# Second attention's front: query and key rows kept token-major, squared and summed on VectorE, normalised along the row, then turned to features

## The chip, the cores and the metric

The kernel runs on one core of a Trainium2 chip. The metric is the device time of one execution in microseconds (us). Engines are written as the profile writes them: PE is TensorE (PEld its weight loads), DVE is VectorE, ACT is ScalarE, POOL is GpSimd, SP is SyncE, which here only issues DMAs.

## The reference, cut to what matters

Two transformer layers run over an input of 8 batches x 512 tokens x 256 features. The change touches only the second layer's attention, with 16 heads of 16 features:

```python
def _rms_norm(x, w):
    ms = jnp.mean(jnp.square(x), axis=-1, keepdims=True)
    return x * jax.lax.rsqrt(ms + EPS) * w
...
xh = x.reshape(b, t, H, HD).transpose(0, 2, 1, 3)
c_q = jnp.einsum('bhtd,ld->bhtl', xh, W_DQ)
q_c = jnp.einsum('bhtl,dl->bhtd', c_q, W_UQ)
q_c_norm = _rms_norm(q_c, q_norm_w)
...
k_c_norm = _rms_norm(k_c, k_norm_w)
k_r = jnp.einsum('bhtd,rd->bhtr', xh, W_KR)
...
scores = jnp.einsum('bhqd,bhkd->bhqk', q, k) * scale
```

The rotary weights are folded into the key side beforehand, so that one query row of 16 features and one key row of 16 features (normalised key plus a linear term of x) give the scores. The mean in the norm goes over the 16 features of one head and one token.

## The kernel before, in words

The second layer (function `layer1`) walks a common list of **slots**. Slot n computes the scores of head n (128 heads, n = 0 to 127), and exponentials, the product with the values and the output of earlier heads. Every engine has its own program, written in slot order, and runs it strictly in that order; engines wait for each other by semaphores.

Beside the heads runs the **front**: front f (16 of them, one for 8 heads of one batch) makes queries, keys and values for 8 heads. Its steps are spread over slots: step s of front f stands in slot 8f - 23 + s (`front_at`, LEAD = 23), so one step of some front with the same remainder by 8 stands in each slot. In the text "slot 4" is a slot that holds step 4 (and step 12 of the front before it). Fronts 0 to 2 stand mostly in slots below 0, where there are no heads yet.

The steps that matter, before the change (a = 0 is the query, a = 1 the key):

- step -2, `turn`, `features`: PE turns x to feature-major, ACT copies it to `xs`.
- steps 1 and 2, `project`: one matmul with 512 columns from fixed weights to `ps_b` (features on partitions, tokens along the row); ACT copies it out (`keep`, to `raw_q` / `raw_k`) and squares it (`square`, to `sq`).
- steps 3 and 5, `squares`: four matmuls against the 128x8 matrix `mean8` give the mean square of each token and head, tokens on partitions; DVE adds the epsilon (`means`, L1988).
- POOL, `root`: to the power -1/2, 16 numbers a partition at a time; step 4 and 5 for the query's two halves, 6 and 7 for the key's. `widen` (steps 5 and 7) copies each root to its head's 16 columns in `roots`.
- `spread_roots` (step 7 query, step 12 key): PE turns `roots` to feature-major in `ps_a`; DVE multiplies (`normed`, L1995, same slots). `rotary` (step 12) adds the key's linear term.
- `high` (ACT) and `low` (DVE) split query (steps 8 and 9) and key (step 13) into a high and a low word; SP writes them out (`spread`) and gathers them by head (`fill`).
- `values` (step 9): PE makes the values from `xs` and may start when the query's multiply is done.

In each slot POOL first cuts the upper triangle from an earlier head's exponentials (`cut`, L1551: two instructions, the second waits for ACT's last exponential of that slot). In each slot DVE first takes the maxima of the slot's four score tiles (`mask_max`, L2019); PE's scores of the next slot wait for them tile by tile. In slots 2 and 6 DVE then runs `outputs` (L2029 to L2036), and PE's `attend` in the following slot (3 or 7) waits for its second instruction. In slots 3 and 8 (until batch 7 is done) DVE runs `mix` (L1974 to L1981), and POOL issues the gathers for it.

## Time and profile before

| | us |
|---|---|
| median of 3 runs | 1800.76 (1798.89 to 1802.2) |
| the profiled execution | 1813.85 |
| its span in the trace | 1812.1 |
| second attention with fronts beside the heads | about 1116 to 1490 of the span |
| busy share of the whole span | PE 91%, DVE 66%, ACT 56%, POOL 30% |

The trace is one execution; its times are microseconds from the start of the span. The busy share of PE is modelled from pipelined matmuls, so durations that follow each other closely overlap; where a cost of PE is wanted, the distance from one start to the next is used.

### The profile page before, as it was taken

Reading aid. Unit: us, or ns where it says so; the run is one execution under the profiler, and the core shown is the slowest. Engines: PE = TensorE matmul, PEld = TensorE weight load, DVE = VectorE, ACT = ScalarE, POOL = GpSimd, SP = SyncE. Lnnn points to the kernel's source line nnn. Section 1 sums busy time; section 2 is a strip of 40 time slices with the busy share of each in tenths; the row PEclk is TensorE's granted clock in tenths of the full one; section 3 lists DMA queues with packets and bytes.
Section 4 is the critical chain, followed back from the end, with each engine's and each line's share of the span. In section 5 each row is a group of like instructions: output and inputs, shape, how many; then the busy total and the mean of one; then the engine's idle time right before and its main releaser. Section 6 shows DMA issues by size and latency. Waiting matters only on the chain. (4 is left out here: it accounts for less than half of the span.)

```text
span 1812.1 us, 30114 instructions
## 1 busy us (share of the span) xinstructions
PE 1646.1 (91%) x9124; PEld 1131.0 (62%) x9125; DVE 1204.8 (66%) x4166; ACT 1013.9 (56%) x2528; POOL 550.7 (30%) x683
## 2 busy tenths in 40 slices
PE   6899999999999999978688877899999988899996
PEld 4667676767676767654577645566666664466665
DVE  1797878787878788727444445778888776134245
ACT  1676767676767676624233362566667665652430
POOL 1000101010101010101444288789988763200001
PEclk9999999999999999989799986899999998999998
DMA  4211111111111111120244426888877777000000
GB/s 109 71 30 47 41 47 42 48 42 47 41 48 37 49 39 36 36 93 1 82 136 135 113 64 130 141 141 133 137 131 133 117 123 118 1 6 18 18 24 29
DMA packets 82766, 128.35 MB, mean 71 GB/s; under 512 B 14784, under 2 KB 40848, under 8 KB 82496
## 3 DMA queue, kind: packets, MB, share of 16 engines
q1 hardware_dynamic: 71232, 100.11, 27.1%
q0 software_dynamic: 9664, 25.93, 6.0%
q8 instruction: 71, 1.16, 0.3%
q10 hardware_dynamic: 1728, 0.55, 0.2%
q14 instruction: 71, 0.58, 0.1%
HBM read 73.59 MB, written 35.65 MB: 60 GB/s over the span
## 5 line engine op out<-in xcount | busy, mean ns | idle before, releaser
L413 ACT ACTIVATE c_probs<-c_probs,a_negmax 128x128 f32<-128x128 f32 (+3 forms) x512 | 279.6, 550 | 0.0
L1867 ACT ACTIVATE c_probs<-a_ps_st 128x384 f32<-128x384 f32 (+1 forms) x384 | 189.9, 526 | 134.0 <-PE a_ps_st L1667 129.6
L418 ACT ACTIVATE c_probs<-a_ps_trans 128x512 f32<-128x512 f32 (+1 forms) x256 | 124.7, 487 | 215.0 <-PE a_ps_trans L331 214.0
L2019 DVE CUSTOM_DVE_ANT_0 a_junk<-a_ps_score,c_mask 128x128 f32<-128x128 f32 (+3 forms) x512 | 220.3, 486 | 35.4 <-PE a_ps_score L1645 28.5
L473 DVE CUSTOM_DVE_ANT_0 c_probs<-a_ps_score,c_mask 128x128 f32<-128x128 f32 (+3 forms) x512 | 219.6, 485 | 19.8 <-PE a_ps_score L315 18.7
L536 POOL TENSOR_SCALAR a_rstd<-a_mv 128x4 f32<-128x4 f32 x8 | 1.8, 230 | 705.8 <-DVE a_mv L503 705.8
L331 PE MATMUL a_ps_trans<-c_ident,c_probs 128*128 128x128 f32 x1280 | 188.6, 278 | 17.7 <-DVE c_probs L490 16.1
L331 PEld LDWEIGHTS a_ps_trans<-c_ident,c_probs 128*128 128x128 f32 x1280 | 147.1, 141 | 87.4 <-issue 39.3
L1501 POOL TENSOR_TENSOR a_ms<-a_ms,c_minus_half 128x16 f32<-128x16 f32 x64 | 187.4, 2931 | 1.8 <-DVE a_ms L1988 1.8
L1667 PE MATMUL a_ps_st<-a_qs,a_ks 128*128 128x512 f32 (+3 forms) x512 | 155.4, 365 | 26.4 <-ACT c_probs L1867 14.4
L314 PE MATMUL a_ps_score<-a_kh,a_qs 128*128 128x128 f32 (+3 forms) x512 | 167.4, 351 | 7.0 <-issue 4.6
L490 DVE TENSOR_SCALAR c_probs<-c_probs,a_recip 128x128 f32<-128x128 f32 (+3 forms) x512 | 164.3, 384 | 4.5
L315 PE MATMUL a_ps_score<-a_kl,a_qs 128*128 128x128 f32 (+3 forms) x512 | 165.3, 323 | 0.0
L344 PE MATMUL a_ps_y<-c_probs,a_latv 128*64 128x512 f32 (+3 forms) x1024 | 153.1, 441 | 0.5 <-ACT c_probs L418 0.5
L1667 PEld LDWEIGHTS a_ps_st<-a_qs,a_ks 128*128 128x128 f32 x512 | 88.2, 193 | 86.5 <-ACT c_probs L1867 45.7
L1551 POOL TENSOR_SCALAR_AFFINE_SELECT c_probs<-c_probs 128x256 f32<-128x256 f32 x256 | 104.1, 422 | 112.1 <-ACT c_probs L1867 111.7
L465 DVE TENSOR_TENSOR a_qlow<-a_ps_q,a_qs 64x512 fp32r<-64x512 f32 x128 | 88.1, 689 | 73.9 <-ACT a_qs L407 71.4
L297 PE MATMUL a_ps_q<-a_xT,a_wqk 128*128 128x512 f32 x256 | 123.0, 603 | 0.0
L1645 PE MATMUL a_ps_score<-a_ks,a_qs 128*128 128x128 f32 (+3 forms) x512 | 117.6, 351 | 2.1 <-DVE a_negmax L2019 1.6
L344 PEld LDWEIGHTS a_ps_y<-c_probs,a_latv 128*64 128x64 f32 x1024 | 68.1, 137 | 81.0 <-issue 70.7
L371 PE MATMUL a_ps_kv<-a_wvo,a_yT 128*128 128x256 f32 x464 | 105.1, 379 | 0.7 <-ACT a_yT L432 0.7
L314 PEld LDWEIGHTS a_ps_score<-a_kh,a_qs 128*128 128x128 f32 x512 | 97.5, 190 | 12.0 <-issue 9.4
(265 smaller groups left out, 3143.4 us busy)
## 6 DMA issues: line engine op xcount, KB each, us to landing
a_qs<-a_qlow SPq DMA_DIRECT2D x128, 128.0 KB, 2.2
bounce<-a_words SPq DMA_DIRECT2D x64, 256.0 KB, 2.0
a_qs<-bounce SPq DMA_DIRECT2D x128, 128.0 KB, 5.7
a_ks<-bounce SPq DMA_DIRECT2D x128, 128.0 KB, 6.3
slot_out<-m_y SPq DMA_DIRECT2D x80, 128.0 KB, 1.7
a_xT<-in_xT SPq DMA_DIRECT2D x8, 512.0 KB
c_X<-in_x SPq DMA_DIRECT2D x8, 512.0 KB
token_rows<-c_X SPq DMA_DIRECT2D x8, 512.0 KB, 5.7
```

The source lines that it names most:

```text
L314: pe.matmul(to, q, kh[b % 2][:, 0:keys], start=True, stop=False)
L315: last = pe.matmul(to, q, kl[b % 2][:, 0:keys], start=False, stop=True)
L331: last = pe.transpose(ps_trans[(3 * n + grp) % 2][:, col:col + P], prob[:, n % 4, QOFF[i] + P * k:QOFF[i] + P * (k + 1)], C.ident[:])
L344: last = pe.matmul(ps_y[LD * c:LD * (c + 1), P * k:L], latv[g // NPAIR % 2][:, k, :], probT[:, (2 * g + c) % 4, at:at + L - P * k], start= ...
L413: act.activation(at, at, ACT.Exp, scale=-1.0, bias=negmax[:, n % 4, i:i + 1], accum_out=rowsum[:, n % 4, i:i + 1]).then_inc(s_exp, 1)
L418: act.activation(probT[:, n % 4, TGCOL[grp]:TGCOL[grp] + TGLEN[grp]], ps_trans[(3 * n + grp) % 2][:, 0:TGLEN[grp]], ACT.Copy).then_inc(s_p ...
L473: dve.tensor_tensor_reduce(out=prob[:, n % 4, QOFF[i]:QOFF[i] + keys], in0=ps_score[grp][:, SCOL[i]:SCOL[i] + keys], in1=C.mask[:, L - key ...
L490: dve.tensor_scalar(at, at, recip[:, n % 4, i:i + 1], None, ALU.mult).then_inc(s_norm, 1)
L1501: pool.tensor_tensor(at, at, C.minus_half[:, 0:2 * HH], ALU.pow).then_inc(s_root, 1)
L1667: last = pe.matmul(ps_st[item % 2][:, col:col + KLEN[c]], KS[u % NQ][:, j, P * c:P * (c + 1)], QS[u % NQ][:, j, P * c:L], start=True, stop ...
L1867: act.activation(probT[:, r8, col:col + width], ps_st[item % 2][:, 0:width], ACT.Exp).then_inc(s_stc, 1)
L2019: dve.tensor_tensor_reduce(out=junk[:, to:to + keys], in0=ps_score[g][:, at:at + keys], in1=C.mask[:, L - keys:L], scale=-1.0, scalar=3.0e ...
```

## The change

Query and key are now projected with tokens on the partitions: `project` uses the four tiles of `xs` as weights and streams the 128 columns of the weight matrix. ACT copies and squares as before, now scaled by 1/4 so that a sum is a mean. `means` is a `tensor_reduce` over 16 columns on DVE. The epsilon moves to POOL, one `tensor_scalar` ahead of each power. `widen`, `squares` and the matrix `mean8` go away. `normed` multiplies along the row in place in `raw_q` / `raw_k`, with the root broadcast over 16 columns; PE then turns the product (`turn_normed`). ACT makes the query's high word straight from `ps_a` with the norm weight as scale, DVE the low word; for the key ACT writes the weighted tile (`weigh`), DVE adds the rotary term.

In slots: `normed` of the query moves on DVE from 7 to 6, that of the key from 12 to 8; `low` of the query from 9 to 8; the key's `means` from 5 to 4; `high` of the query on ACT from 8 to 7; `weigh` is new in 12. `normed` waits for both halves of POOL's roots; `turn_normed` waits for `normed`; `values` now waits for `low` of the query.

```diff
                 def root(f, a, half):
-                    pool.wait_ge(s_msc, f * 2 + a + 1)
                     at = ms[:, a, 2 * half:2 * half + 2, :].rearrange("p t h -> p (t h)")
+                    pool.wait_ge(s_ms, f * 2 + a + 1)
+                    pool.tensor_scalar(at, at, RMS_EPS, None, ALU.add).then_inc(s_root, 1)
+                    pool.wait_ge(s_root, 8 * f + 4 * a + 2 * half + 1)
                     pool.tensor_tensor(at, at, C.minus_half[:, 0:2 * HH], ALU.pow).then_inc(s_root, 1)
...
+                def project(f, a):
+                    if a:
+                        pe.wait_ge(s_rawc, 2 * f + 1)
+                    else:
                         pe.wait_ge(s_xs, f + 1)
...
+                    for t in range(TT):
+                        last = pe.matmul(ps_b[:, P * t:P * (t + 1)], xs[f % 2][:, P * t:P * (t + 1)],
+                                         w[:, (SQ, SK)[a], :], start=True, stop=True)
+                    last.then_inc(s_raw, 1)
...
                 def values(f):
-                    pe.wait_ge(s_fin, 2 * f + 1)
+                    pe.wait_ge(s_lo, 2 * f + 1)
...
+                def turn_normed(f, a):
+                    pe.wait_ge(s_nrm, f * 2 + a + 1)
...
+                        last = pe.transpose(ps_a[:, P * t:P * (t + 1)], raw(f, a)[:, P * t:P * (t + 1)], C.ident[:])
                     last.then_inc(s_bc, 1)
...
+                        act.activation(words[0][:], ps_a[:], ACT.Copy, scale=qk_norm[:, 0:1]).then_inc(s_hi, 1)
...
+                def weigh(f):
+                    act.wait_ge(s_bc, 2 * f + 2)
...
+                    act.activation(fin, ps_a[:], ACT.Copy, scale=qk_norm[:, 1:2]).then_inc(s_kw, 1)
...
                 def means(f, a):
...
+                    dve.wait_ge(s_sq, f * 2 + a + 1)
+                    dve.tensor_reduce(ms[:, a, :, :].rearrange("p t h -> p (t h)"),
+                                      sq[:, a, :].rearrange("p (n d) -> p n d", d=HD), AX.X, ALU.add
+                                      ).then_inc(s_ms, 1)
 
                 def normed(f, a):
...
+                    dve.wait_ge(s_root, 8 * f + 4 * a + 4)
+                    at = raw(f, a)[:].rearrange("p (t h d) -> p t h d", t=TT, h=HH)
+                    dve.tensor_tensor(at, at, ms[:, a, :, :].unsqueeze(3).to_broadcast([P, TT, HH, HD]),
+                                      ALU.mult).then_inc(s_nrm, 1)
...
                     if front_at(n, 3) is not None:
                         means(front_at(n, 3), 0)
                     if front_at(n, 12) is not None:
-                        normed(front_at(n, 12), 1)
                         rotary(front_at(n, 12))
-                    if front_at(n, 5) is not None:
-                        means(front_at(n, 5), 1)
-                    if front_at(n, 7) is not None:
-                        normed(front_at(n, 7), 0)
-                    if front_at(n, 9) is not None:
-                        low(front_at(n, 9), 0)
+                    if front_at(n, 4) is not None:
+                        means(front_at(n, 4), 1)
+                    if front_at(n, 6) is not None:
+                        normed(front_at(n, 6), 0)
+                    if front_at(n, 8) is not None:
+                        normed(front_at(n, 8), 1)
+                        low(front_at(n, 8), 0)
```

What stands in a row on DVE from the end of slot 6's maxima on, before (each "128x512" row of `c_mask` is the last tile of a slot's maxima, the first tiles are left out; `a_raw_q` is the query, `a_raw_k` the key, `a_got` the mix):

```order
L2019 ISA a_junk,a_negmax<-a_ps_score,c_mask 128x512
...
L2029 RECIPROCAL a_recip<-a_ps_y 128x16
L2031 TENSOR_TENSOR a_yq<-a_ps_y,a_recip 128x256
L2036 TENSOR_TENSOR c_X<-c_X,a_yq 128x4x64
...
L1995 SCALAR_TENSOR_TENSOR a_sq<-a_raw_q,c_qk_norm,a_ps_a 128x512
L2043 BN_STATS a_stats<-c_X 128x6
...
L1974 SCALAR_TENSOR_TENSOR c_X<-a_got,c_weight,c_X 128x256 x2
```

The same stretch of DVE after the change:

```order
L2001 ISA a_junk,a_negmax<-a_ps_score,c_mask 128x512
...
L1977 TENSOR_TENSOR a_raw_q<-a_raw_q,a_ms 128x512
L2011 RECIPROCAL a_recip<-a_ps_y 128x16
L2013 TENSOR_TENSOR a_yq<-a_ps_y,a_recip 128x256
L2018 TENSOR_TENSOR c_X<-c_X,a_yq 128x4x64
...
L2025 BN_STATS a_stats<-c_X 128x6
...
L1977 TENSOR_TENSOR a_raw_k<-a_raw_k,a_ms 128x512
L1936 SCALAR_TENSOR_TENSOR a_words<-a_ps_a,c_qk_norm,a_words 128x512
L1959 SCALAR_TENSOR_TENSOR c_X<-a_got,c_weight,c_X 128x256 x2
```

The query's multiply now stands ahead of slot 6's `outputs`, and the key's multiply and the query's low word stand between slot 8's maxima and its mix.

POOL from slot 4 to slot 8, before:

```order
L1501 TENSOR_TENSOR a_ms<-a_ms,c_minus_half 128x16
L1551 AFFINE_SELECT c_probs<-c_probs 128x2x128 x2
L1501 TENSOR_TENSOR a_ms<-a_ms,c_minus_half 128x16
L1507 COPY a_roots<-a_ms 128x512
L1551 AFFINE_SELECT c_probs<-c_probs 128x2x128 x4
```

and after:

```order
L1499 TENSOR_SCALAR a_ms<-a_ms 128x16
L1501 TENSOR_TENSOR a_ms<-a_ms,c_minus_half 128x16
L1543 AFFINE_SELECT c_probs<-c_probs 128x2x128 x2
L1499 TENSOR_SCALAR a_ms<-a_ms 128x16
L1501 TENSOR_TENSOR a_ms<-a_ms,c_minus_half 128x16
L1543 AFFINE_SELECT c_probs<-c_probs 128x2x128 x4
```

This is the key's half (slots 6 to 8); the query's reads alike. The copy after two powers is gone, and each power has an addition ahead of it.

## Rows read from the trace of the kernel before

**Rows 1.** Windows view: stretch, length, busy us (instructions), PEclk, DMA share, GB/s
```profile
1200.00:1300.00 100.00, 93.49 (x669) 61.62 (x668) 82.98 (x321) 67.51 (x142) 88.86 (x108) 1.00 0.83 135
```
**Rows 2.** Windows view of PE alone: stretch, length, busy us (instructions), PEclk, DMA share, GB/s
```profile
1504.00:1508.00 4.00, 2.38 (x10) 0.85 0.61 101
1508.00:1512.00 4.00, 4.00 (x20) 0.73 1.11 123
```
**Rows 3.** Waits view from 1165 to 1480: us in total, times, longest us
```profile
PEld a_ps_a L1633 <- POOL a_roots L1507: 19.7, 12, 1.8
```
**Rows 4.** Chain of work that ended last, merged: start us, us, what
```profile
1286.69 0.89 PE a_ps_a L1602 x8
1287.58 0.86 PE a_ps_b L1596 x2
...
1294.98 0.79 PE a_ps_a L1617 x8
```
**Rows 5.** Timeline of POOL: start us, us, instruction xcount [idle before <-releaser]
```profile
1070.15 5.82 POOL L1501 TENSOR_TENSOR a_ms<-a_ms,c_minus_half 128x16 f32<-128x16 f32 x2
...
1083.14 0.59 POOL L1524 TENSOR_SCALAR a_crstd<-a_cmv 128x4 f32<-128x4 f32 x1
...
1291.00 0.23 POOL L1524 TENSOR_SCALAR a_crstd<-a_cmv 128x4 f32<-128x4 f32 x1
1291.32 1.04 POOL L1526 TENSOR_TENSOR a_crstd<-a_crstd,c_minus_half 128x4 f32<-128x4 f32 x1
...
1301.33 2.94 POOL L1501 TENSOR_TENSOR a_ms<-a_ms,c_minus_half 128x16 f32<-128x16 f32 x1
...
1304.98 2.90 POOL L1501 TENSOR_TENSOR a_ms<-a_ms,c_minus_half 128x16 f32<-128x16 f32 x1
1307.94 0.61 POOL L1507 COPY a_roots<-a_ms 128x512 f32<-128x512 f32 x1
...
1313.02 3.06 POOL L1501 TENSOR_TENSOR a_ms<-a_ms,c_minus_half 128x16 f32<-128x16 f32 x1
```
**Rows 6.** Timeline of DVE, slots 6 to 9
```profile
1306.01 0.42 DVE L2031 TENSOR_TENSOR a_yq<-a_ps_y,a_recip 128x256 f32<-128x256 f32 x1
...
1309.30 0.75 DVE L1995 SCALAR_TENSOR_TENSOR a_sq<-a_raw_q,c_qk_norm,a_ps_a 128x512 f32<-128x512 f32 x1 [0.59 <-PE a_ps_a L1633]
1309.97 0.42 DVE L2043 BATCH_NORM_STATS2 a_stats<-c_X 128x6 f32<-128x256 f32 x1
...
1310.54 0.29 DVE L2019 CUSTOM_DVE_ANT_0 a_junk<-a_ps_score,c_mask 128x128 f32<-128x128 f32 x1
...
1312.19 1.14 DVE L1974 SCALAR_TENSOR_TENSOR c_X<-a_got,c_weight,c_X 128x256 f32<-128x256 f32 x2
...
1313.94 0.29 DVE L2019 CUSTOM_DVE_ANT_0 a_junk<-a_ps_score,c_mask 128x128 f32<-128x128 f32 x1
...
1315.59 0.69 DVE L1951 TENSOR_TENSOR a_words<-a_sq,a_words 128x512 fp32r<-128x512 f32 x1
1316.20 0.42 DVE L2043 BATCH_NORM_STATS2 a_stats<-c_X 128x6 f32<-128x256 f32 x1
```
**Rows 7.** Timeline of PE: slot 2's scores, slot 7's attend, then slots 8 to 10
```profile
1288.89 0.85 PE L1645 MATMUL a_ps_score<-a_ks,a_qs 128*128 128x128 f32 x4
...
1306.70 1.07 PE L1683 MATMUL a_ps_y<-c_probs,a_v 128*32 128x512 f32 x8
...
1308.61 0.66 PE L1633 MATMUL a_ps_a<-c_ident,a_roots 128*128 128x128 f32 x4 [0.84 <-POOL a_roots L1507]
...
1309.28 0.85 PE L1645 MATMUL a_ps_score<-a_ks,a_qs 128*128 128x128 f32 x4
...
1312.69 0.86 PE L1645 MATMUL a_ps_score<-a_ks,a_qs 128*128 128x128 f32 x4
...
1313.79 1.05 PE L1602 MATMUL a_ps_a<-c_w,a_xs 128*128 128x128 f32 x8
...
1316.15 0.85 PE L1645 MATMUL a_ps_score<-a_ks,a_qs 128*128 128x128 f32 x4
```

146 lines of the change are left out of this document (51 added, 95 removed).

## The prediction, as it was put on record

> **What bounds the kernel now.** I read the windows first, then the waits, the chain of work, and the timelines of POOL, DVE and PE over one front's period. From 1200 to 1300, beside the heads, PE is busy 93.49 of 100 us, POOL 88.86, DVE 82.98 and ACT 67.51, at a full PE clock [rows 1]. Three engines are near their limit, so what counts is who waits for whom in order. One front with its eight heads takes 27.26 us: slot 2's scores start at 1288.89, and those of slot 10 (the next slot 2) at 1316.15 [rows 7]. PE is the bound most of the time, but the period closes through POOL: between 1165 and 1480 PE's weight loads stand 19.7 us, 12 times, for the widened roots [rows 3]. POOL's four powers are the long piece: each is 2.9 us, they start at 1301.33, cannot start earlier (they stand behind a cut that waits for slot 4's last exponential), and the last one ends at 1313.02 + 3.06 = 1316.08 [rows 5]. That is the time at which PE is already in slot 10. Nobody minds today, because the key's roots are used only in slot 12.
>
> **PE.** Removed per front: two `squares` of 0.79 us [rows 4]. Two projections of 0.86 us become eight token tiles; their nearest row is `values`, four tiles of the same shape in 0.89 us [rows 4], so +0.03 each. The turns stay eight transposes. Sum: 1.58 - 0.06 = 1.52 us less on PE a front, 24 us in 16 fronts, if PE stays the bound.
>
> **POOL.** The addition ahead of each power costs 0.32 us from start to start, by the addition of 4 numbers that stands at 1291.00 ahead of a power at 1291.32 [rows 5]; with 16 numbers it may be 0.4. The copy that goes cost 1308.52 - 1307.94 = 0.58 plus 0.06 ahead of it (the copy starts at 1307.94 behind a power at 1304.98 of 2.90, the next cut follows it directly [rows 5]). Four additions, two copies: 1.28 against 1.28, nothing, at worst +0.3. Counted from the start of the first power's addition (R), the query's roots are ready at 0.32 + 2.92 + 0.73 (a cut of two instructions: 1304.98 - 1301.33 - 2.92 [rows 5]) + 0.32 + 2.88 = 7.2, the key's at 4 x 3.22 + 3 x 0.76 = 15.15.
>
> **DVE's own work.** `means` grows from 0.11 (start to start, 128x32) to about 0.6: not shown before; bounds 0.43 (half the elements) and 0.75, nearest row a 512-element operation, 0.61 from start to start (1315.59 to 1316.20 [rows 6]). `normed` shrinks from 0.67 (1309.97 - 1309.30) to 0.61, `low` of the query grows from 0.61 to 0.67. Together +0.95 us a front. DVE is idle 17 of 100 us, 4.6 a front, so this work alone costs nothing; if it fell on the path in full it would be 13 x 0.95 = 12. ACT gets `weigh`, 0.6 us in slot 4; it is idle 32 of 100 us [rows 1], nothing either.
>
> **DVE's new place in the order.** Here the time is decided. DVE runs in order, and `normed` now waits for POOL inside the stream of maxima on which PE's scores depend. I take R = 1301.33 and give times after R.
>
> Slot 6: DVE is through with its maxima at 4.4 (`outputs` begins with a reciprocal 0.28 ahead of 1306.01) and waits until 7.2 for the query's roots. Behind it stand `outputs`, whose second instruction PE's `attend` in slot 7 wants. Before it started at 1306.01, ended at 1306.43, and `attend` started at 1306.70 [rows 6, 7]: there was no slack at all. Now 7.2 + 0.61 + 0.74 = 8.55 and `attend` starts 3.2 us later than its 5.37. One thing comes back: the 0.84 us for which the turn at 1308.61 waited. From `attend` to slot 8's scores it was 1309.28 - 1306.70 = 2.58, without that wait 1.7 [rows 7]; slot 8's scores start at 10.2 instead of 7.95.
>
> Slot 8: DVE takes slot 7's maxima from 9.05 to 10.7, statistics 0.57 (1310.54 - 1309.97), slot 8's maxima 1.65 (1312.19 - 1310.54 [rows 6]) to 12.9, and then waits for the key's roots until 15.2. `normed` to 15.8, `low` to 16.5, the mix 1.75 (1313.94 - 1312.19) to 18.2, slot 9's maxima to 19.85. PE: slot 9's scores at 10.2 + 3.41 = 13.6, `values` could start 1.10 later, at 14.7 (1313.79 - 1312.69 [rows 7]), but waits for `low` until 16.5: 1.8 us. From `values` to slot 10 it is 1316.15 - 1313.79 = 2.36: slot 10 at 18.9, where its last tile waits for the last maximum at 19.9. That equals a start at 19.5 without waits. Before it was 1316.15 - 1301.33 = 14.8. So the stretch from the roots to slot 10 is 4.7 us longer while there is a mix, 4.1 without.
>
> The rest of the period, slot 2's scores to the next R, was 1301.33 - 1288.89 = 12.44 and loses one `squares`: 11.65. Period 19.5 + 11.65 = 31.15, **3.9 us more than 27.26**; without the mix 3.3. The other `squares` (slot 5) and PE's 1.5 us are swallowed by the waits.
>
> **Sum.** Fronts 4 to 12 have the mix and a full period: 9 x 3.9 = 35. Fronts 13 and 14: 2 x 3.3 = 7. Front 15 pays 4.1 and has no next one. Front 3, whose last two powers stand behind the first cuts, pays 4.4 - 0.8 = 3.6. Ahead of the heads the same wait delays the mix: front 0's powers start at 1070.15, four of 3.22 end at 1083.05, then 0.61 + 0.67 + 1.6 (mix) bring the statistics to 1086.0, for which POOL waits with what began at 1083.14 [rows 5]: 2.9 us. Front 2 does it again and holds up slots 2 to 4, about 3 more: 6, between 2 (PE waits for a DMA ahead of slot 7's exponents, which could hide most of it) and 9. Together 35 + 7 + 4.1 + 3.6 + 6 = **56 us**. The profiled execution would go from 1813.85 to 1870; the median of the runs lies 13.1 lower, so 1800.76 + 56 = **1857**.
>
> **A rule beside it.** POOL's power was 2.90 us in most rows and 3.06 beside the mix at 1312.19, a DVE instruction with two inputs from SBUF [rows 5, 6]. The new `normed` of the query is another such instruction and meets POOL's cut and third power: by 3.06 - 2.90 some 0.15 us a front, 2 us in all. The Trainium skill (GPSIMD Engine Reference, section Key points) says that GPSIMD shares its SBUF interfaces with VectorE and contends with instructions that have two SBUF inputs; by that rule the sum would be 58 instead of 56. I keep 56.
>
> **The rivals.**
> *A, the clock (22%).* With 7 us of PE waits in a period of 31, PE's clock may fall. In a stretch of 4 us of the trace before in which PE was busy for 2.38, the granted clock was 0.85, and 0.73 in the next 4, PE being partly at 1.2 instead of 2.4 GHz [rows 2]: (0.15 + 0.27) x 4 = 1.7 us lost. Once a front on the path: 13 x 1.7 = 22, 1879. Against it: half of the waits stand ahead of PE work that has slack until `low`. The Trainium skill (TensorE: Matmul & The Clock Gate, section HAM oscillation) warns that waits between bursts of matmuls make the clock fall again each time; by it this rival would be the likely one.
> *B, partly absorbed (14%).* PE reaches slot 4 early enough that the pattern settles with 1.5 to 2.5 us a front: 13 x 2 + 3 = 29, 1830. It needs slots 10 to 12 to run faster than before; DVE's 0.95 us speak against it.
> *C, faster (7%).* DVE's waits never reach PE and PE's relief counts: 1801 - 24 = 1777. The point that decides: the key's roots must be ready when DVE is through with slot 8's maxima. Before that was at 1312.19, and POOL's last power ended at 1316.08: 3.9 us too late, with POOL no faster than before.
> *D, no difference (5%).* The new waits cost just the 1.5 us a front that PE saves, 1801.
> The forecast has 52%.
>
> **How the numbers follow.** Predicted is the likeliest case, 1857, whose own range is 1843 to 1871 (the startup from 2 to 9, the addition, the reduce, the mix). The range takes in rival A and the upper half of B: 1832 to 1885. A measurement of this kernel can tell about 0.2%, 3.6 us. Faster: C and a little, 0.08. Same: 0.05. Slower: 0.87.
>
> **What would show it.** In the profile after: DVE waiting for POOL at `normed`, about 2.8 us in slot 6 and 2.3 in slot 8 of each front; PE waiting ahead of `attend` in slot 7 (3.2 us) and ahead of `values` (1.8); the distance between two fronts' first powers 31 us with the mix; POOL idle longer ahead of slot 4's cut; PE busy below 80 of 100 us between 1200 and 1300. Wrong it would be if DVE found the roots ready (the roots' place on POOL moved forward), if the reduce took over 1.2 us (DVE would be the bound), or if slots 10 to 12 ran at a different pace. A granted clock well below 1.00 there speaks for A.

## The result, and the profile after

| | before | after |
|---|---|---|
| median, first chip | 1799.83 us (4 runs, 1797.65 to 1802.2) | 1884.84 us (4 runs, 1883.24 to 1888.08) |
| ratio, 95% interval | | 1.0474 (1.0458 to 1.0489) |
| ratio, second chip (a0_again) | 1812.16 us | 1897.48 us, 1.0465 (1.0447 to 1.0482) |
| span of the profiled execution | 1812.1 us | 1886.4 us |

The change makes the kernel 4.7% slower: 85 us, where 56 was forecast (1857, range to 1885). Against the 1800.76 of the prediction the ratio gives 1886.1, a hair outside the range. The sign and the waits were as predicted; the size was a third too small, mainly because TensorE's clock was taken as staying full.

Two stretches of the windows view of the profile after; the columns are those of [rows 1].

```profile
core 0: us, PE busy (x) PEld busy (x) DVE busy (x) ACT busy (x) POOL busy (x), PEclk, DMA share, GB/s
1200.00:1300.00 100.00, 80.70 (x555) 52.68 (x548) 72.35 (x265) 57.15 (x118) 74.49 (x93) 0.91 0.68 114
...
1400.00:1500.00 100.00, 78.67 (x520) 53.45 (x519) 68.61 (x257) 57.16 (x119) 66.97 (x85) 0.90 0.59 101
```

From 1200 to 1300 every engine does less than in [rows 1] (PE 93.49, DVE 82.98, ACT 67.51, POOL 88.86), and the granted clock is 0.91 where it was 1.00. No engine has become the bound. They wait for one another.

Who waits for whom, from 1165 to 1540 (us in total, times, longest). There are 11 rounds of a front here.

```profile
POOL c_probs L1543 <- ACT c_probs L1847: 91.7, 58, 5.3
...
PE a_ps_y L1661 <- DVE a_yq L2013: 41.6, 11, 4.8
DVE a_raw_q L1977 <- POOL a_ms L1501: 34.6, 11, 4.1
DVE a_raw_k L1977 <- POOL a_ms L1501: 28.4, 11, 3.1
...
PE a_ps_a L1598 <- DVE a_words L1936: 14.7, 11, 1.7
```

Rows three and four are the new ones: VectorE stands 3.1 us a front at the query's roots and 2.6 us at the key's (forecast 2.8 and 2.3). Row two is what follows: TensorE's `attend` waits 3.8 us a front for the outputs that are queued behind the first of these waits. Row five is the values' wait for the low half. In [rows 3] the longest of TensorE's waits for roots was 1.8 us.

One front in the timelines of POOL, DVE and PE, beside [rows 5 to 7]. The first power's addition starts at 1203.44; times "after R" are counted from there.

```profile
1203.44 0.26 POOL L1499 TENSOR_SCALAR a_ms<-a_ms 128x16 f32<-128x16 f32 x1
1203.78 2.94 POOL L1501 TENSOR_TENSOR a_ms<-a_ms,c_minus_half 128x16 f32<-128x16 f32 x1
1206.70 0.76 POOL L1543 TENSOR_SCALAR_AFFINE_SELECT c_probs<-c_probs 128x256 f32<-128x256 f32 x2
...
1207.78 2.94 POOL L1501 TENSOR_TENSOR a_ms<-a_ms,c_minus_half 128x16 f32<-128x16 f32 x1
1210.69 1.21 POOL L1543 TENSOR_SCALAR_AFFINE_SELECT c_probs<-c_probs 128x256 f32<-128x256 f32 x2
...
1212.21 2.93 POOL L1501 TENSOR_TENSOR a_ms<-a_ms,c_minus_half 128x16 f32<-128x16 f32 x1
1215.11 0.41 POOL L1543 TENSOR_SCALAR_AFFINE_SELECT c_probs<-c_probs 128x256 f32<-128x256 f32 x1
1216.62 0.41 POOL L1543 TENSOR_SCALAR_AFFINE_SELECT c_probs<-c_probs 128x256 f32<-128x256 f32 x1 [1.10 <-ACT c_probs L1847]
...
1217.34 2.93 POOL L1501 TENSOR_TENSOR a_ms<-a_ms,c_minus_half 128x16 f32<-128x16 f32 x1
1220.24 1.21 POOL L1543 TENSOR_SCALAR_AFFINE_SELECT c_probs<-c_probs 128x256 f32<-128x256 f32 x2
```

```profile
1210.75 0.88 DVE L1977 TENSOR_TENSOR a_raw_q<-a_raw_q,a_ms 128x512 f32<-128x512 f32 x1 [2.94 <-POOL a_ms L1501]
...
1211.83 0.42 DVE L2013 TENSOR_TENSOR a_yq<-a_ps_y,a_recip 128x256 f32<-128x256 f32 x1
...
1220.30 0.88 DVE L1977 TENSOR_TENSOR a_raw_k<-a_raw_k,a_ms 128x512 f32<-128x512 f32 x1 [2.30 <-POOL a_ms L1501]
1221.11 0.74 DVE L1936 SCALAR_TENSOR_TENSOR a_words<-a_ps_a,c_qk_norm,a_words 128x512 fp32r<-128x512 f32 x1
```

```profile
1212.40 1.93 PE L1661 MATMUL a_ps_y<-c_probs,a_v 128*32 128x512 f32 x8 [3.58 <-DVE a_yq L2013]
1214.27 1.12 PE L1611 MATMUL a_ps_a<-c_ident,a_raw_q 128*128 128x128 f32 x4
...
1215.50 1.48 PE L1623 MATMUL a_ps_score<-a_ks,a_qs 128*128 128x128 f32 x4
...
1221.90 1.16 PE L1598 MATMUL a_ps_a<-c_w,a_xs 128*128 128x128 f32 x8 [0.75 <-DVE a_words L1936]
...
1224.41 0.62 PE L1623 MATMUL a_ps_score<-a_ks,a_qs 128*128 128x128 f32 x3
```

The query's roots end at 1210.72, 7.3 after R. VectorE, idle for 2.94 us, starts at once. The second instruction of the outputs ends at 1212.25 and `attend` starts at 1212.40. In slot 7 POOL's second cut waits 1.10 us for ScalarE's exponential (1216.62), so the key's roots end at 1220.27, 16.8 after R. The low half ends at 1221.85 and the values start at 1221.90. The scores of slot 10 start at 1224.41, 21.0 after R; before, it was 14.8 from the first power [rows 5, 7].

The granted clock of the same stretch, in the windows view of PE alone (length, busy us, PEclk, DMA share, GB/s):

```profile
1204.00:1208.00 4.00, 3.36 (x22) 1.00 0.38 139
1208.00:1212.00 4.00, 0.82 (x4) 0.90 0.95 141
1212.00:1216.00 4.00, 3.60 (x16) 0.50 1.04 120
1216.00:1220.00 4.00, 4.00 (x34) 0.74 0.23 73
```

TensorE was busy for 0.82 of the 4 us from 1208 to 1212. In the next four the clock is 0.50 (1.2 instead of 2.4 GHz) and then 0.74. That is why `attend` takes 1.93 us here instead of 1.07, the turn 1.12 instead of 0.66 and the scores 1.48 instead of 0.85. The Trainium skill (TensorE: Matmul & The Clock Gate, section HAM oscillation) says that waits between bursts of matmuls make the clock fall again each time; this trace agrees: from front 4 to front 15, `attend` in slot 7 takes 1.86 to 1.94 us in each of the twelve rows. It is not so in every trace. In a0_again, the same kernel run once more, one of these rows takes 1.49 us, and two (fronts 6 and 11) are at full speed, behind waits of 2.27 us:

```profile
1251.77 1.06 PE L1661 MATMUL a_ps_y<-c_probs,a_v 128*32 128x512 f32 x8 [2.27 <-DVE a_yq L2013]
```

Fronts 11 to 13 have a second fall, behind the values' wait (PE timeline of front 12):

```profile
1456.89 2.01 PE L1598 MATMUL a_ps_a<-c_w,a_xs 128*128 128x128 f32 x8 [1.74 <-DVE a_words L1936]
...
1461.03 0.84 PE L1623 MATMUL a_ps_score<-a_ks,a_qs 128*128 128x128 f32 x4
```

The values take 2.01 us instead of 1.16, and slot 10's scores start 23.1 us after that front's first addition (1437.96). The three rounds that begin with such a front are 34.0 to 34.5 us long, the others 32.7 to 34.3.

Two distances summarise a run. The **start** is the time from the first power of front 0 to the first power of front 4. The **period** is the mean distance of first powers from front 4 to front 15, eleven rounds.

| | start | period | total |
|---|---|---|---|
| before | 94.1 | 27.35 | 94.1 + 300.8 = 394.9 |
| after | 106.4 | 33.53 | 106.4 + 368.9 = 475.3 |

That is 80 us more (84 in the trace of a0_again). From the last front's first power to the end it is 347.0 us before and 346.7 after, so nothing is lost or won later. The whole spans are only 74 us apart, because front 0's first power starts at 1070.2 before and at 1064.4 after. In a0_again, the same kernel as after, it starts at 1070.4, so these 6 us are not the change's doing.

### The profile page after: what moved, and what is told of

Read it like the earlier page. It is cut to its first block and busy times, and to the rows that moved or that the text cites. A ratio compares the mean times of both kernels' runs of the same rounds, so it can differ in the third digit from the quotient of the medians.

```text
span 1886.4 us, 29928 instructions
## 1 busy us (share of the span) xinstructions
PE 1650.7 (88%) x9060; PEld 1138.2 (60%) x9061; DVE 1223.9 (65%) x4166; ACT 1024.1 (54%) x2544; POOL 561.3 (30%) x715
## 3 DMA queue, kind: packets, MB, share of 16 engines
q8 instruction: 71, 1.16, 0.3%
## 5 line engine op out<-in xcount | busy, mean ns | idle before, releaser
L2001 DVE CUSTOM_DVE_ANT_0 a_junk<-a_ps_score,c_mask 128x128 f32<-128x128 f32 (+3 forms) x512 | 220.2, 486 | 46.3 <-PE a_ps_score L1623 41.7
L1645 PE MATMUL a_ps_st<-a_qs,a_ks 128*128 128x512 f32 (+3 forms) x512 | 157.7, 374 | 20.5 <-ACT c_probs L1847 14.4
L1543 POOL TENSOR_SCALAR_AFFINE_SELECT c_probs<-c_probs 128x256 f32<-128x256 f32 x256 | 114.4, 456 | 172.7 <-ACT c_probs L1847 172.2
L1645 PEld LDWEIGHTS a_ps_st<-a_qs,a_ks 128*128 128x128 f32 x512 | 92.0, 200 | 77.4 <-ACT c_probs L1847 47.4
L1661 PE MATMUL a_ps_y<-c_probs,a_v 128*32 128x512 f32 (+3 forms) x1024 | 92.5, 481 | 45.2 <-DVE a_yq L2013 45.2
L1623 PE MATMUL a_ps_score<-a_ks,a_qs 128*128 128x128 f32 (+3 forms) x512 | 125.1, 364 | 5.7 <-DVE a_negmax L2001 3.8
```

What stands on the lines that cost most here:

```text
L1623: last = pe.matmul(ps_score[g][:, SCOL[i]:SCOL[i] + keys], QS[u % NQ][:, j, P * i:P * (i + 1)], KS[u % NQ][:, j, 0:keys], start=True, stop ...
L1645: last = pe.matmul(ps_st[item % 2][:, col:col + KLEN[c]], KS[u % NQ][:, j, P * c:P * (c + 1)], QS[u % NQ][:, j, P * c:L], start=True, stop ...
L2001: dve.tensor_tensor_reduce(out=junk[:, to:to + keys], in0=ps_score[g][:, at:at + keys], in1=C.mask[:, L - keys:L], scale=-1.0, scalar=3.0e ...
```

## The experiments

All ratios are to the kernel before, measured on the same chip (1810.3 to 1812.3 us there); 0.001 is 1.8 us. "Query" and "key" give the slot step in which VectorE calls `normed`, and whether it stands ahead of the outputs (step 6) or behind them.

| kernel | what | ratio | 95% interval | start | period |
|---|---|---|---|---|---|
| a0_again | query 6 ahead, key 8 (the change) | 1.0465 | 1.0447 to 1.0482 | 106.3 | 33.9 |
| e1_key_late | key 11 | 1.0231 | 1.0204 to 1.0259 | 93.7 | 31.5 |
| e2_query_behind | query 6 behind | 1.0419 | 1.0399 to 1.0439 | 106.7 | 33.2 |
| e3_both | both | 1.0107 | 1.0077 to 1.0136 | 93.8 | 29.3 |
| s1_shifted | query 7 behind, key 11, readers a slot later | 0.9943 | 0.9926 to 0.9960 | 91.3 | 26.9 |
| s2_key_early | s1, key 8 | 1.0458 | 1.0440 to 1.0475 | 105.7 | 33.5 |
| s3_query_early | s1, query 6 ahead | 1.0265 | 1.0248 to 1.0282 | 93.1 | 31.6 |
| p1_short_chain | the change, half of the powers left out | 0.9951 | 0.9934 to 0.9967 | 92.3 | 27.3 |
| c1_values_late | the change, values at 10 | 1.0459 | 1.0441 to 1.0476 | 105.4 | 33.9 |
| b1_waits_only | before + two waits | 1.0238 | 1.0221 to 1.0255 | 99.0 | 30.5 |
| b4_waits_and_work | b1 + a multiply behind each | 1.0346 | 1.0322 to 1.0370 | 103.4 | 31.5 |
| e4_fill | the change, PE busy ahead of attend | 1.0422 | 1.0402 to 1.0443 | 106.5 | 32.7 |
| e7_fill_both | also ahead of the values | 1.0378 | 1.0340 to 1.0417 | 106.4 | 32.5 |
| e8_key_late_fill | e1 + e4 | 1.0147 | 1.0109 to 1.0185 | 93.6 | 30.0 |
| s5_shift_add_on_dve | s1, additions on VectorE | 0.9945 | 0.9928 to 0.9962 | 90.6 | 27.3 |
| s6_turn_cover | s1, turn a slot earlier | 1.0002 | 0.9993 to 1.0012 | 92.7 | 28.0 |

### Is it the wait, or the work, or the place?

**p1_short_chain** leaves the normalisations where the change put them and shortens what they wait for.

```diff
-                    pool.tensor_tensor(at, at, C.minus_half[:, 0:2 * HH], ALU.pow).then_inc(s_root, 1)
+                    if half:
+                        pool.tensor_scalar(at, at, 0.0, 0.05, ALU.mult, ALU.add).then_inc(s_root, 1)
+                    else:
+                        pool.tensor_tensor(at, at, C.minus_half[:, 0:2 * HH], ALU.pow).then_inc(s_root, 1)
```

> The changed kernel with the second of each pair of powers on GpSimd (half the tokens of each front's query and key) replaced by one instruction that writes a constant: half of the roots are left out, everything else runs in the same order. The power took 2.94 us, a GpSimd instruction with a scalar on 16 numbers 0.26. VectorE's waits stay where the change put them, but what they wait for comes sooner: the query's roots 2.7 us, the key's 5.4 us. Theory 1 (VectorE standing in order at GpSimd's chain): both waits (2.9 and 2.3 us) nearly vanish and the time falls to 0.985 to 1.005 of the kernel before, with the two normalisations still at steps 6 and 8. A rival, the place itself (the normalisation ahead of the outputs and the low half is late whatever GpSimd does): 1.02 or more.

Measured: 0.9951, faster than the kernel before, with both normalisations at steps 6 and 8 and half of the roots left out. VectorE's waits for POOL, from 1165 to 1540:

```profile
DVE a_raw_q L1980 <- POOL a_ms L1502: 4.6, 11, 1.4
DVE a_raw_k L1980 <- POOL a_ms L1502: 3.6, 11, 0.8
```

From 34.6 and 28.4 us they are down to 4.6 and 3.6. So the place is harmless by itself, and so are the reduction, the turn and the low half in slot 8. What costs is that the roots are not there yet. This kernel also takes 5.4 us a front of POOL's work away; that it is not this which helps is shown by s1 below, which keeps all four powers and runs as fast.

**b1_waits_only** puts nothing but the two waits into the kernel before.

```diff
+                    if front_at(n, 6) is not None:
+                        dve.wait_ge(s_root, 4 * front_at(n, 6) + 2)
                     if front_at(n, 12) is not None:
                         normed(front_at(n, 12), 1)
...
+                    if front_at(n, 8) is not None:
+                        dve.wait_ge(s_root, 4 * front_at(n, 8) + 4)
                     if front_at(n, 9) is not None:
                         low(front_at(n, 9), 0)
```

> The kernel before the change, with two waits added on VectorE and nothing else: in the slot of step 6, ahead of rotary, VectorE waits for GpSimd's query roots, and in that of step 8, ahead of the low half, for the key's roots. The same work is computed. Theory 1 (in-order VectorE standing at the roots is the cause): 1800 + 16 x 3.5 to 5.5 = 1856 to 1888 us, though here no normalisation takes VectorE's time behind the wait. Theory 3 (the added work is the cause, and the waits are absorbed): 1798 to 1810 us.

Measured: 1.0238, 43 us, and 30.45 us a front. Half of the loss comes back with two waits that compute nothing. Theory 1 had expected 56 to 88 us, too much.

**b4_waits_and_work** adds a multiply behind each wait, of the shape of the new normalisation, into a tile that nothing reads.

```diff
+                    if front_at(n, 6) is not None:
+                        dve.wait_ge(s_root, 4 * front_at(n, 6) + 2)
+                        dve.wait_ge(s_spare, 2 * front_at(n, 6) + 0 + 1)
+                        dve.tensor_tensor(spare[:]..., spare[:]..., ms[:, 0, :, :]..., ALU.mult)
...
```

> The kernel before the change, with the two added waits of b1_waits_only on VectorE and, behind each, a multiply of 128x512 numbers from SBUF by the roots, into a tile that nothing reads: the shape of the new normalisation. b1 had 30.45 us a front against 27.35 before and 33.5 in the changed kernel, so the bare waits are half of the loss. Theory 1a (the rest is the normalisation's own 0.7 to 0.9 us behind each wait, on the path, with what it does to the clock): 32 to 33 us a front, 1.0238 + 16 x 1.5 to 2.5 / 1810 = 1.037 to 1.046 of before. Theory 1b (the rest lies elsewhere: the values that now wait for the low half one slot earlier, the reductions, the additions on GpSimd): within 0.005 of b1, up to 1.029.

Measured: 1.0346. The multiplies are worth another 20 us (0.0346 - 0.0238), 1.1 us a front and 4.4 us in the start. That is just short of theory 1a (1.037). Not all of it is their own time. With the multiply in front of it, `attend` waits up to 2.6 us instead of 2.0, and the clock falls behind that wait in six of twelve rounds, where b1 has one slow `attend`:

```profile
1213.67 1.94 PE L1685 MATMUL a_ps_y<-c_probs,a_v 128*32 128x512 f32 x8 [2.60 <-DVE a_yq L2033]
```

How the 20 us divide between the two is not shown. Of the change's 84 us (0.0465 x 1811) this pair leaves 22.

### Each place by itself

**e1_key_late, e2_query_behind, e3_both** move the calls on VectorE.

```diff
# e1 (e3 has both)
+                    if front_at(n, 11) is not None:
+                        normed(front_at(n, 11), 1)
                     if front_at(n, 3) is not None:
                         means(front_at(n, 3), 0)
...
                     if front_at(n, 8) is not None:
-                        normed(front_at(n, 8), 1)
                         low(front_at(n, 8), 0)
# e2
-                    if front_at(n, 6) is not None:
-                        normed(front_at(n, 6), 0)
...
                         outputs((n - 15) // QUAD)
+                    if front_at(n, 6) is not None:
+                        normed(front_at(n, 6), 0)
```

> The changed kernel, with one edit: on VectorE the key's normalisation is called in the slot of step 11, ahead of the means, instead of step 8, ahead of the low half. The same work is computed. Theory 1 (VectorE standing at the key's roots holds back the words of the other attention that are queued behind it): the wait of 2.3 us before the key's reduction goes, the low half of slot 8 no longer stands behind it, and values and slot 10's scores come some 2 to 3 us earlier in each of 16 fronts: 1885 - 16 x 2.0 to 2.8 = 1840 to 1853 us. Theory 2 (the fall of TensorE's granted clock after the query's wait is the larger part): the query's wait is untouched, so the clock still falls, and at most the 0.7 us by which values wait go: 1865 to 1885 us. Theory 3 (the added VectorE and GpSimd instructions and their contention set the time, wherever they stand): no change, 1880 to 1888 us.

> The changed kernel, with one edit: in the slot of step 6 the query's normalisation on VectorE stands behind the other attention's outputs instead of ahead of them. The same work is computed. Theory 1: attend in slot 7 no longer waits 3.58 us for the output rows that VectorE holds behind the wait for the query's roots; TensorE's halves keep the high granted clock there; what is then late is only the turn of the normalised query and the scores behind it, by 1 us or so. That gives back 1.5 to 3 us in each of 16 fronts: 1837 to 1861 us. Theory 2 gives more than the wait alone, as the 1.5 to 1.9 us of the halved clock come back too: down to 1830 us, and the mean granted clock goes from 0.946 to 0.96 or more. Theory 3: no change, 1880 to 1888 us.

> The changed kernel with both edits together: the key's normalisation in the slot of step 11, and the query's behind the outputs in that of step 6. The same work is computed. Theory 1: nearly all that the change costs goes, and the relief of TensorE by the projections that it no longer repeats can show: 1775 to 1810 us, and the period of a front on TensorE is 27 to 28 us instead of 32.8. Theory 2: likewise, with the granted clock at 0.96 or more. Theory 3: 1870 us or more. If the two single edits add up, this one is within 10 us of 1885 less both gains; if one wait takes the place of the other, it gains more than the two singly.

Measured: moving the key alone gives back 42 us (1.0465 to 1.0231), 12.6 of them in the start. Moving the query alone gives back 8. Moving both gives 65. The two single gains add up to 50, so together they give more than singly. The expectation for e2 (24 to 48 us, and a mean clock of 0.96) was wrong: its mean clock is 0.945, like the change's 0.946. For e1 theory 1 had the right size; e3 missed its band, since 29.3 us a front is not 27 to 28. In e2 the waits of TensorE and of VectorE from 1165 to 1540 read:

```profile
PE a_ps_a L1598 <- DVE a_words L1936: 27.3, 11, 3.1
PE a_ps_a L1611 <- DVE a_raw_q L1977: 19.2, 11, 3.3
DVE a_raw_k L1977 <- POOL a_ms L1501: 41.5, 11, 4.2
DVE a_raw_q L1977 <- POOL a_ms L1501: 23.3, 11, 3.5
```

`attend` no longer waits. But the turn of the normalised query now stands 1.7 us a front for VectorE (row two), and the values' wait for the low half has grown from 14.7 to 27.3 us (row one). VectorE stands less at the query's roots (23.3 us instead of 34.6) and longer at the key's (41.5 instead of 28.4); the sum is 64.8, against 63.0 in the change. That is the larger lesson, and two kernels that put one place back into the best version show it plainly.

**s1_shifted, s2_key_early, s3_query_early.** The first has both normalisations late and gives their readers a slot more.

```diff
# s1, against the change
 PE:  values at step 10 (was 9), turn_normed of the query at 8 (was 7)
 ACT: keep_values at 10 (was 9), high of the query at 8 (was 7)
 DVE: normed(., 0) at 7 behind outputs (was 6, ahead), low at 9 (was 8), normed(., 1) at 11 (was 8)
# s2, against s1
+                    if front_at(n, 8) is not None:
+                        normed(front_at(n, 8), 1)
# s3, against s1
+                    if front_at(n, 6) is not None:
+                        normed(front_at(n, 6), 0)
```

> The changed kernel with its front re-timed: the query's normalisation on VectorE at step 7 behind the outputs, its turn and high half at step 8, the low half at step 9, the values and their eviction at step 10, the key's normalisation at step 11, its turn and what follows as before. The same work is computed. Theory 1: no engine stands at the roots any more, and TensorE, with its 16 x 1.5 us of projections less, is the bound: 1772 to 1792 us, faster than the kernel before (1800). Theory 3 (VectorE's and GpSimd's added work is on the path): 1830 us or more. Another way: the scores of slot 8 wait for the high half instead, and it lands at 1795 to 1810 us.

> The re-timed kernel s1_shifted (0.9943), with the key's normalisation on VectorE back at step 8, where the change has it; the low half (step 9) and the values (step 10) stay a slot later than in the change. The same work is computed. With s3_query_early (1.0265) it prices the second of the two places by itself. Theory 1: VectorE stands in slot 8 for the key's roots, which end some 16 us after the first power's start, and slot 9's maxima and the mix come late; ahead of the heads the mix is held back as well (12.7 us by the kernel with the key late): 1.012 to 1.022. If only the readers of the low half had been the trouble: 0.994 to 1.004.

> The re-timed kernel s1_shifted (0.9943 of the kernel before), with the query's normalisation on VectorE back at step 6, ahead of the outputs, where the change has it; its readers stay a slot later. The same work is computed. It prices the query's place alone, where no reader of it is near. Theory 1: VectorE stands 2.5 to 3 us at the query's roots, attend waits for the outputs behind it as in the changed kernel, and 2 to 3 us a front are lost: 0.994 + 16 x 2 to 3 / 1810 = 1.012 to 1.021. Theory of the readers (what costs is that turn and high half need the result in slot 7, not that VectorE stands): 0.994 to 1.000.

Measured: **s1 runs in 0.9943 of the kernel before, 1801.4 us beside 1810.3**, and so beats both kernels. One front of it, DVE and then PE; R is 1217.51:

```profile
1222.08 0.42 DVE L2013 TENSOR_TENSOR a_yq<-a_ps_y,a_recip 128x256 f32<-128x256 f32 x1
...
1224.82 0.88 DVE L1977 TENSOR_TENSOR a_raw_q<-a_raw_q,a_ms 128x512 f32<-128x512 f32 x1
```

```profile
1222.80 1.06 PE L1661 MATMUL a_ps_y<-c_probs,a_v 128*32 128x512 f32 x8
...
1224.08 1.25 PE L1623 MATMUL a_ps_score<-a_ks,a_qs 128*128 128x128 f32 x4
```

The query's product starts 7.3 after R, at the same time as in the change. But the outputs have gone ahead of it (4.6 after R instead of 8.4), so `attend` starts at 5.3 and runs at the full clock. The windows view of s1 from 1200 to 1300, columns as above, has the clock at 1.00:

```profile
1200.00:1300.00 100.00, 89.91 (x664) 60.35 (x653) 87.88 (x322) 71.44 (x148) 90.70 (x117) 1.00 0.80 136
```

By the ratio that is 1790 us on the first chip, within theory 1's 1772 to 1792, at its slow end.

Each early place alone undoes it, and more than expected: s3 costs 0.0322, 58 us, and s2 0.0515, 93 us, while both together, in the change (where the readers also stand a slot earlier), cost 95. The costs do not add. s2's rows say why (DVE, then PE; R is 1208.80):

```profile
1216.12 0.88 DVE L1977 TENSOR_TENSOR a_raw_q<-a_raw_q,a_ms 128x512 f32<-128x512 f32 x1 [0.21 <-POOL a_ms L1501]
...
1224.55 0.88 DVE L1977 TENSOR_TENSOR a_raw_k<-a_raw_k,a_ms 128x512 f32<-128x512 f32 x1 [5.90 <-POOL a_ms L1501]
```

```profile
1227.83 1.89 PE L1623 MATMUL a_ps_score<-a_ks,a_qs 128*128 128x128 f32 x4 [4.86 <-DVE a_negmax L2001]
```

VectorE has only 0.21 us to wait for the query, is through with slot 8's maxima 9.9 after R instead of 14.6, and stands there for **5.90 us** instead of 2.30. From 1165 to 1540 it stands 4.7 us for the query and 59.7 for the key, 64.4 in all; in the change it was 34.6 + 28.4 = 63.0. The key's roots end 15.7 after R, whenever VectorE arrives. The next scores on TensorE wait 4.86 us for a maximum, and the clock falls behind that wait as well: these scores take 1.89 us instead of 0.85, and 1.88 to 2.01 us in each of the eleven rounds. In s3 `attend` is slow (1.29 to 1.94 us) in eleven rounds of twelve. So the 93 and the 58 each hold a fall of the clock; the change has one fall a front for both places together, which is part of why the costs do not add. The end of POOL's fourth power is an appointment: an earlier wait taken away ahead of it only makes the wait at it longer. This is why e2 gained so little, and, with the clock, why the 32 to 50 us that I expected for s2 were about half of the measured 93.

**c1_values_late** moves the values and their eviction to step 10 in the change.

```diff
-                    if front_at(n, 9) is not None:
-                        values(front_at(n, 9))
+                    if front_at(n, 10) is not None:
+                        values(front_at(n, 10))
```

> The changed kernel with only the values of the front and their eviction moved from step 9 to step 10. The same work is computed. In the changed kernel the values wait on TensorE for the query's low half, which stands on VectorE behind the key's roots; the kernel before had no such wait. The kernel before with both bare waits and a multiply behind each (1.0346) leaves 0.012 of the change's 1.0465 unexplained, some 21 us. If the values' wait is that piece, 1.034 to 1.038; if it is only 0.75 us a front of it, 1.040 to 1.043; if slot 9's maxima and what stands behind the key's wait are late anyway, no change (1.045 to 1.048).

Measured: 1.0459 against 1.0465, no difference. It fits the appointment: with the values out of the way, slot 9's maxima are still behind the same wait.

### The clock

**e4_fill, e7_fill_both, e8_key_late_fill** keep TensorE busy in its waits with matmuls whose result is not used.

```diff
+                    if front_at(n, 7) is not None and n >= 12:
+                        if front_at(n, 7) >= 1:
+                            pe.wait_ge(s_fin, front_at(n, 7))
+                        for _ in range(3):
+                            pe.matmul(ps_b[:], w[:, SG, :], xs[front_at(n, 7) % 2][:], start=True, stop=True)
                     if n >= 12 and n % QUAD == 0 and (n - 12) // QUAD < NQUADS:
                         attend((n - 12) // QUAD, (0,))
```

> The changed kernel with three more matmuls of 512 columns on TensorE in the slot of step 7, ahead of attend, once a front; their results are not used, and nothing waits for them. They take 0.65 us together at the high clock and fall into the 3.58 us in which TensorE stands before attend. It tells apart how much the fall of the clock costs: theory 2 (attend's halves, the turn and the scores at the halved clock are 1.5 to 1.9 us late on the path that sets the end) expects the clock to stay up behind the wait and 1885 - 16 x 1.5 to 1.9 = 1855 to 1861 us; if the clock falls all the same, or if what comes behind waits for another engine anyway, 1880 to 1890 us.

> The changed kernel with TensorE kept busy in both of its long waits of a front: the three matmuls of 512 columns ahead of attend as in e4_fill (they took 2.73 us there, not the 0.65 that I had written), and two more ahead of the values in slot 9; their results are not used. In e4_fill the scores of slot 8 came 1.4 us sooner, but the clock then fell behind the values' wait: values, projection and transposes took 1.68, 1.91 and 0.95 us instead of 1.16, 1.06 and 0.60, and slot 10's scores started 21.5 us after the first power's addition instead of 21.0. If the two falls together are the part of the loss that the prediction left out, this kernel has 31 to 32 us a front instead of 33.9, and 1.030 to 1.038 of the kernel before, against 1.0422 with one fill and 1.0465 without. If the time goes by the appointments with GpSimd alone, 1.040 to 1.044; if the added matmuls themselves come late, slower than e4_fill.

> The changed kernel with the key's normalisation in the slot of step 11 (as e1_key_late, 1.0231) and the three unused matmuls ahead of attend (as e4_fill). Only the query's wait is left, and TensorE is busy in it, so what is left over 0.9943 of the re-timed kernel is the wait itself without the clock. If the fall of the clock behind attend is worth 1.4 us a front once the key's appointment no longer follows it: 1.0231 - 16 x 1.0 to 1.4 / 1811 = 1.011 to 1.014. If the wait alone is the price: 1.020 to 1.024.

PE in one front of e4; R is 1209.16:

```profile
1214.39 2.73 PE L1724 MATMUL a_ps_b<-a_xs,c_w 128*128 128x512 f32 x6
1218.14 1.07 PE L1661 MATMUL a_ps_y<-c_probs,a_v 128*32 128x512 f32 x8 [1.01 <-DVE a_yq L2018]
1219.13 0.66 PE L1611 MATMUL a_ps_a<-c_ident,a_raw_q 128*128 128x128 f32 x4
...
1219.80 0.85 PE L1623 MATMUL a_ps_score<-a_ks,a_qs 128*128 128x128 f32 x4
...
1226.50 1.68 PE L1598 MATMUL a_ps_a<-c_w,a_xs 128*128 128x128 f32 x8 [1.90 <-DVE a_words L1941]
1227.96 1.91 PE L1587 MATMUL a_ps_b<-c_w,a_xs 128*128 128x128 f32 x8
...
1230.64 0.86 PE L1623 MATMUL a_ps_score<-a_ks,a_qs 128*128 128x128 f32 x4
```

(The three matmuls took 2.73 us and not the 0.65 of my expectation; they still fit into the wait.) `attend`, the turn and the scores run in 1.07, 0.66 and 0.85 us, and slot 8's scores start 10.6 after R instead of 12.1. But then the values wait 1.90 us instead of 0.75, the clock falls behind that wait (1.68, 1.91), and slot 10's scores start at 21.5, no sooner than in the change. In this front the fall has only moved; so it is in one other (1.79 us) and in part in a third (1.34), and in the rest e4 keeps what it won: 32.7 us a front against 33.9. Its 1.0422 is 8 us, short of the 24 to 30 that theory 2 expected. With both waits filled (e7), no front from 4 on has slow values and only one a slow `attend` (1.92 us), the period is 32.5, and the ratio goes from 1.0465 to 1.0378, 16 us. With the only remaining wait filled (e8), e1 goes from 1.0231 to 1.0147, 15 us. The ratios of e7 and e8 lie at and just above the top of what they were expected to be if the clock counts (1.038 and 1.014); e7's period was expected at 31 to 32. Both differences of ratios are uncertain by about 8 us. The periods of the traces say 1.45 and 1.56 us a front, 16 and 17 in eleven fronts.

### The best version

> The re-timed kernel s1_shifted, with the four additions of 16 numbers on GpSimd (0.34 us each from start to start) replaced by two of 32 numbers on VectorE behind the reductions (0.1 us each in the kernel before). The same work is computed. In s1 GpSimd was busy 93.6 and VectorE 90.8 of 100 us from 1300 to 1400, TensorE 91.7. If GpSimd's chain of powers and cuts sets the 27.3 us of a front beside the mix, 0.5 to 1.2 us a front come back and it lands at 0.985 to 0.990 of the kernel before; if TensorE or VectorE sets it, it stays at 0.994 or is a little slower.

```diff
-                    pool.wait_ge(s_ms, f * 2 + a + 1)
-                    pool.tensor_scalar(at, at, RMS_EPS, None, ALU.add).then_inc(s_root, 1)
+                    pool.wait_ge(s_msc, f * 2 + a + 1)
...
+                    dve.tensor_scalar(at, at, RMS_EPS, None, ALU.add).then_inc(s_msc, 1)
```

> The re-timed kernel s1_shifted (0.9943), with TensorE's turn of the next front's input moved from step -2 to step -3, that is from slot 6 to slot 5. The same work is computed. In s1 TensorE stands 1.07 us in slot 5 ahead of the transposes of the outputs until ScalarE has copied them; in the kernel before the squares of the key stood ahead of them and covered that wait, so the relief of TensorE is eaten there. With the turn (0.6 us) in their place the wait should shrink to 0.4 us and the period by up to 0.6 us, 16 x 0.3 to 0.6: 0.989 to 0.992. If ScalarE or VectorE (87.9 to 90.8 busy) closes the period: 0.994.

```diff
-                    if front_at(n, -2) is not None:
-                        turn(front_at(n, -2))
+                    if front_at(n, -3) is not None:
+                        turn(front_at(n, -3))
```

Neither helps. s5 measured 0.9945: four additions of 0.34 us less a front on POOL, and two more on VectorE, change nothing, so it does not seem to be POOL that closes s1's period. s6, expected at 0.989 to 0.992, measured 1.0002, slower than s1 by 0.006. TensorE's waits in it, from 1165 to 1540:

```profile
PE a_ps_y L1670 <- ACT a_yq L1873: 13.8, 23, 1.4
PE a_ps_a L1575 <- ACT c_X L1853: 12.8, 5, 2.6
```

The turn now comes before ScalarE has written its input: up to 2.6 us, five times, once for each new batch of tokens. The wait that it was to cover is 13.8 us over 23 times; in s1 it was 19.8 over 25.

## Why the prediction was right and wrong

| step, after R | predicted | measured, R = 1203.44 |
|---|---|---|
| query's roots end | 7.2 | 7.3 |
| `attend` | 8.55 | 8.96 |
| scores of slot 8 | 10.2 | 12.06 |
| key's roots end | 15.15 | 16.83 |
| `values` | 16.5 | 18.46 |
| scores of slot 10 | 18.9, worth 19.5 | 20.97 |
| from there to the next R | 11.65 | 11.87 |
| period | 31.15 | 32.84; 33.5 on average |
| eleven periods, more than before | 9 x 3.9 + 2 x 3.3 = 41.7 | 68 |
| start, more than before | 6 + 3.6 = 9.6 | 12.3 |
| last front | 4.1 | 0 |

**Right: the mechanism of the waits.** VectorE in order, standing at POOL's roots in slots 6 and 8, with `attend`, the maxima and the values queued behind. p1 (shorter chain, no loss), b1 (waits alone, 43 us) and s1 (same work without the waits, faster than before) show it from three sides. The waits on VectorE had nearly the predicted lengths (3.1 and 2.6 us on average, 2.8 and 2.3 predicted); `attend` waited 3.8 us instead of 3.2, the values 1.3 instead of 1.8. The start was nearly right too, and it belongs to the key's wait: with the change's front, the key at step 8 and POOL's whole chain it is 105 to 107 us, with the key at 11 it is 91 to 94.

**Wrong: the clock was taken as staying full.** The forecast priced the fall at nothing and kept it as rival A: once a front, 1.7 us, 22 us in all, at 22%. It came, once a front and in three fronts twice. e7 and e8 put it at 15 to 16 us, each uncertain by about 8. It belonged into the sum: a wait of 3.2 us on TensorE ahead of `attend` was itself a step of that sum, and [rows 2] had shown what the clock does behind a thin stretch.

**Wrong: POOL's chain was taken as unbroken.** "The key's at 4 x 3.22 + 3 x 0.76" assumed that each cut finds its exponentials ready. In the change the second cut of slot 7 waits 1.10 us for ScalarE, whose exponential is late because the scores were, because the clock was. So a delay of TensorE behind the first wait comes back as a later appointment at the second. In e4, with the clock up, the same two cuts take 0.77 us without a gap and the roots end 15.7 after R. It is so in every front: from the first power's start to the end of the last, fronts 4 to 15 take 16.4 to 17.0 us in the change and 15.3 to 15.7 in e4 (in the kernel before 14.4 to 14.8), and in a0_again 15.4 in just the two fronts in which `attend` ran at full speed.

**Mis-sized: VectorE and POOL side by side.** I gave the meeting of the new multiply with POOL 0.15 us a front, beside the sum and not in it, and only for the query's. The multiply takes 0.88 us in 25 of its 32 runs, all beside a pair of cuts, and 0.68 or 0.69 in the seven without, and POOL's pair of cuts beside it 1.21 us instead of 0.76. Twice a front that is 2 x 0.2 on VectorE; the first pair of cuts also makes the third power 0.45 us late, which is nearly the rest from 15.15 to 15.7. The rule that I set beside the sum (the Trainium skill, GPSIMD Engine Reference, section Key points: contention with instructions that have two SBUF inputs) agrees with these rows; I had taken its price from a row in which the two hardly met.

**Also off.** The last front's 4.1 us were not paid: 346.7 us to the end against 347.0. Of the relief of TensorE, put at 24 us, only s1, s5 and p1 show any. s1's 0.9943 is 10 us; its TensorE stands 19.8 us from 1165 to 1540 ahead of the outputs' transposes (L1670) where the kernel before stood 9.8, probably since the removed `squares` had covered part of that wait. What the reduction and the smaller `means` cost was right at nothing.

**The sum again.** From front 0's first power to the end the traces differ by 80 us, and 56 were forecast. The last front's 4.1 were not paid, and the start took 2.7 more. In the eleven periods the clock adds 15 to 16 (e7, e8) and the contention, by an estimate from the rows above that no run has tested by itself, at most 0.85 us a front (0.45 + 2 x 0.2), 9 in all. That makes 79 to 80. The medians differ by 85. The pieces overlap through the appointment, so this agreement is no proof of each. One piece stays open. b4, with its two multiplies, has a period of 31.5 although its clock falls in half of the rounds, and e7 has 32.5 with the clock held up nearly throughout, so at least 1 us a front lies elsewhere. c1 rules out the values' place alone, and nothing here tells the turn and high half in slot 7 from the additions on POOL.

## What to carry to other kernels

When a step moves to an in-order engine ahead of work that others need, ask when its input will be ready, not when the engine is free. If the input's producer has a fixed schedule, two waits for it do not add: moving the earlier one away gave back 8 us here, the later one 42, both 65, so begin with the last. Put the consumer as many slots behind the producer as its length needs, and behind everything in its slot that someone else waits for: here one to three slots turned 4.7% slower into 0.6% faster. And where a forecast gives TensorE a wait in each round as long as the one here (3.6 us ahead of `attend`), price the halved clock behind it into the sum, with what it does to the engines that come next.

## What the runs showed of the hardware

- Who pays when VectorE and POOL meet depends on what POOL does. In the change the multiply of 128x512 with both inputs in SBUF took 0.88 us each time that a pair of cuts began with it, and the pair took 1.21 us instead of 0.76; in s1 it took 0.86 to 0.93 in nearly all such cases. Beside a power, or while POOL issued a gather, the multiply took 0.68 or 0.69; three powers that began beside it took 3.19 us instead of 2.94.
- The reduction of 128x512 numbers over groups of 16 took 0.68 us, just as long as a VectorE multiply of that size (0.69).
- POOL's addition to 16 numbers a partition took 0.26 us and the power behind it started 0.34 after it; the power took 2.93 or 2.94 us in 59 of 64 cases (3.19 at most).
- Behind a wait of TensorE ahead of `attend` the clock fell in all twelve fronts of the change (waits of 3.57 to 4.79 us), but not in all of a0_again, and in e1 one `attend` ran in 1.06 us behind a wait of 3.57. Filling this wait kept the clock up there (e4: 1.06 or 1.07 us in every front); in two of eleven fronts, and in part in a third, it then fell at the next one.
